# Decoder attention pass: both logits ahead of the guard's transform, a second key buffer, context energy on TensorE and variance on ScalarE

## The reference

```python
x = _layernorm(x + _L0_attn_ref(x), axis=-1)                     # autocorrelation, top 7 lags of 2048
x = _layernorm(x + _L0_xattn_ref(ctx_4096, ctx_4096, x), axis=-1)
x = _layernorm(x + _L0_ffn_ref(x, W_base, gate_W, A, B), axis=-1)

# _L0_xattn_ref(key, value, query)
sim = jnp.einsum('ncs,nds->ncd', key, query) * KC ** (-0.5)      # KC = 256
sim = jax.nn.softmax(sim, axis=1)
context = jnp.einsum('ncd,nds->ncs', sim, value)

# _L0_ffn_ref: a dense product and a mixture of low-rank experts
out = xf @ W_base.T + _moe_lora(xf, gate_W, A, B)                # 8 experts, rank 8, top 2
```

## Time and profile before

| | us |
|---|---|
| median of three runs | 2191.81 |
| the profiled execution | 2195.65 |
| its span, first to last instruction | 2193.8 |
| attention, up to the reading of the guard's flag | about 721 |

### The profile page before, as it was taken

One profiled execution on the slowest core, in us unless ns is written; L12 is line 12 of the kernel. 1 busy time (PEld: TensorE's weight loads), 2 busy tenths in 40 slices (PEclk: granted clock), 3 DMA queues, 4 the chain that ended last, 5 costly groups with the idle time before them and its releaser, 6 DMA issues.

```text
span 2193.8 us, 27988 instructions
## 1 busy us (share of the span) xinstructions
PE 1990.9 (91%) x11232; PEld 1056.9 (48%) x11232; DVE 988.7 (45%) x2182; ACT 511.9 (23%) x691; POOL 296.7 (14%) x418
## 2 busy tenths in 40 slices
PE   1878878878888699999999999999999999999998
PEld 1655645555555344444444444444444444444443
DVE  3788878888887652232223222232223222232222
ACT  4445444544442540010001000010001000110000
POOL 1242243243242320000000000000000000000000
PEclk9999999998999799999999999999999999999999
DMA  7588678778866752232223322232223322232220
GB/s 250 135 220 256 215 205 241 245 198 233 251 184 191 256 158 58 59 105 65 57 57 91 81 58 57 65 103 62 57 57 96 76 57 57 71 100 59 57 58 39
DMA packets 288907, 271.13 MB, mean 124 GB/s; under 512 B 261504, under 2 KB 261632, under 8 KB 265984
## 3 DMA queue, kind: packets, MB, share of 16 engines
q1 hardware_dynamic: 288832, 270.17, 42.4%
HBM read 138.02 MB, written 67.11 MB: 94 GB/s over the span
## 4 chain that ended last, share of the span: by engine, by line
PE 64%; ACT 1%; DMA 1%; POOL 1%; DVE 0%; issue 0%; ACTq 0%; SPq 0%; POOLq 0%
PE ps_y_f L1097 59%; PE ps_a_f L1116 1%; PE ps_y_f L1101 1%; PE ps_y_f L1102 1%; DMA chunk<-w_chunks 1%; PE ps_a_f L1117 1%; ACT w_hi_f L892 1%; POOL w_lo_f L875 0%; POOL chunk L874 0%; DVE w_lo_f L966 0%; PE ps_h_f L1124 0%; PE ps_t_f L1082 0%; DVE b_stack_f L1052 0%; ACT y_f L953 0%; ACT b_stack_f L950 0%
## 5 line engine op out<-in xcount | busy, mean ns | idle before, releaser
L1097 PE MATMUL ps_y_f<-w_hi_f,x_hi_f 128*128 128x512 f16 x2048 | 777.8, 380 | 9.9 <-POOL w_lo_f L875 7.4
L1097 PE MATMUL ps_y_f<-w_hi_f,x_lo_f 128*128 128x512 f16 x2048 | 778.0, 380 | 0.0
L1097 PE MATMUL ps_y_f<-w_lo_f,x_hi_f 128*128 128x512 f16 x2048 | 777.9, 380 | 0.0
L953 ACT ACTIVATE y_f<-y_f,nb_f,rs_f 128x2048 f32<-128x2048 f32 x32 | 67.0, 2093 | 1112.4 <-POOL nb_f L883 1112.4
L1097 PEld LDWEIGHTS ps_y_f<-w_hi_f,x_hi_f 128*128 128x128 f16 x2048 | 200.7, 98 | 246.8 <-POOL w_lo_f L875 9.6
L1097 PEld LDWEIGHTS ps_y_f<-w_hi_f,x_lo_f 128*128 128x128 f16 x2048 | 200.8, 98 | 242.6 <-issue 1.6
L1097 PEld LDWEIGHTS ps_y_f<-w_lo_f,x_hi_f 128*128 128x128 f16 x2048 | 200.7, 98 | 233.9 <-issue 1.4
L977 DVE SCALAR_TENSOR_TENSOR y_f<-ps_y_f,w_iscale,xn_f 128x512 f32<-128x512 f32 x64 | 46.6, 749 | 476.9 <-PE ps_y_f L1102 476.9
L977 DVE SCALAR_TENSOR_TENSOR y_f<-ps_y_f,w_iscale,xn 128x512 f32<-128x512 f32 x64 | 46.6, 748 | 447.9 <-PE ps_y_f L1102 447.9
L610 PE MATMUL ps_t_fast<-ident,xbuf_fast 128*128 128x128 f32 x512 | 95.5, 334 | 134.1 <-ACT xbuf_fast L413 116.3
L880 POOL TENSOR_TENSOR var_eps_f<-mv_f,columns 128x1 f32<-128x1 f32 x32 | 6.1, 191 | 1356.9 <-DVE mv_f L1065 1356.9
(11 more groups left out here) (146 smaller groups left out, 2055.2 us busy)
## 6 DMA issues: line engine op xcount, KB each, us to landing
cbuf_fast<-ctx_in SPq DMA_DIRECT2D x32, 1024.0 KB, 6.1
xbuf_fast<-x SPq DMA_DIRECT2D x32, 1024.0 KB, 8.8
x_scratch<-x2buf_fast SPq DMA_DIRECT2D x32, 1024.0 KB, 11.7
out<-y_f SPq DMA_DIRECT2D x32, 1024.0 KB, 4.1
xn<-w_chunks SPq DMA_DIRECT2D x16, 1024.0 KB, 8.4
xn<-x_scratch SPq DMA_DIRECT2D x16, 1024.0 KB, 4.8
xn_f<-x_scratch SPq DMA_DIRECT2D x16, 1024.0 KB, 4.8
chunk<-w_chunks SPq DMA_DIRECT2D x18, 512.0 KB, 5.6
```

The costliest lines, as they stand in the source:

```text
L953: nc.scalar.activation(y[parity][:], y[parity][:], ACT.Identity, bias=nb_[:, 0:1], scale=rs[:, 0:1]).then_inc(out_ready, 1)
L1097: nc.tensor.matmul(ps_y[j][:], xx[parity][:, k], ww[:, k, j * BANK:(j + 1) * BANK], start=(k == 0 and xx is x_hi and ww is w_hi), stop=False)
```

## The change

- The all-reduce of the context's squares (`reduce_context`, GpSimd) is replaced by one matmul with a matrix of ones (`context_energy`, TensorE, after the last bank of transposes). Its result of four columns lies in the PSUM bank of logits(1), so logits(1) waits for the scale.
- `k_both` has two buffers. The transposes of batch n + 2 stand at the end of slot n and wait for logits of batch n. In SP's queue the order of a slot is now store, weights, x, transposes with context n + 3.
- TensorE runs logits(0), logits(1), then the guard's transform and its way back.
- The statistics of x2 are no longer bn_stats. The context addition on VectorE also writes the sum of its output (`x2sum`), `x2_mean` makes the mean, ScalarE squares the centred rows with their sum (`spread2`), and GpSimd makes the normalisation from it, each row tile for itself (`norm2`, `normalise2`). For r = 1 this lies in the next slot.
- The first normalisation goes by row tile too: `norm_steps` twice, and `normalise1` for both tiles on ScalarE, the second one last in its slot.
- ScalarE's order after the banks: v_hi twice, normalise1(0), exponential(0), two squares of weights, exponential(1), four guard squares, normalise1(1).
- Some buffers share memory: `u_t` lies in `ag_raw`, one context buffer in two of the prefetched weight chunks. So the prefetches at the end of attention wait for the last transform and the last v_lo.

```diff
-                        transpose_keys(n + 1, 1 - parity, 0, 0)
-                        transpose_keys(n + 1, 1 - parity, 0, 1)
-                        for r in range(R):
-                            transpose_keys(n + 1, 1 - parity, 1, r)
-                            load_context(n + 2, r)
+                        store(n - 1, 1 - parity)
                         load_weights(n + 2)
-                        store(n - 1, 1 - parity)
                         load_x(n + 2, parity)
+                    for r in range(R):
+                        transpose_keys(n + 2, parity, 0, r)
+                    for r in range(R):
+                        transpose_keys(n + 2, parity, 1, r)
+                        load_context(n + 3, r)
...
                         if (part, r) == (0, 0):
-                            after(sp, sim_done, R * n)
+                            after(sp, sim_done, R * (n - 1))
...
+                def norm2(n, parity, r):
+                    at = slice(r, r + 1)
+                    pool.wait_ge(ssq2_ready, R * n + r + 1)
...
+                def normalise2(n, parity, r):
+                    pool.wait_ge(ln2_ready, R * n + r + 1)
...
+                    if is_batch(n - 1, nb):
+                        norm2(n - 1, 1 - parity, 1)
+                        normalise2(n - 1, 1 - parity, 1)
+                    if cur and n < nb - 1:
+                        norm2(n, parity, 0)
+                        normalise2(n, parity, 0)
+                    fold(0)
+                    norm1(0)
+                    fold(1)
+                    norm1(1)
...
+                    def spread2(n, parity, r):
+                        act.wait_ge(mean2_ready, R * n + r + 1)
+                        after(act, ssq2_ready, R * n + r)
+                        nc.scalar.activation(junk2[:], x2buf[parity][:, r], ACT.Square, bias=nmean2[parity][:, r:r + 1],
+                                             accum_out=ssq2[parity][:, r:r + 1]).then_inc(ssq2_ready, 1)
...
+                        if j == 1 and is_batch(n - 1, nb):
+                            spread2(n - 1, other, 1)
+                        if j == 5 and cur:
+                            spread2(n, parity, 0)
...
                                                    xbuf[parity][:, r, b * BANK:(b + 1) * BANK], ALU.mult,
-                                                   ALU.add).then_inc(ctx_added, 1)
-                            if j:
-                                x2_stats(j - 1)
+                                                   ALU.add, accum_out=x2sum[:, j:j + 1]).then_inc(ctx_added, 1)
+                            if j == NBANK:
+                                x2_mean(0)
...
                     softmax_max(0)
                     x_stats(1)
+                    guard_lags(0)
                     softmax_norm(0)
-                    guard_lags(0)
+                    softmax_max(1)
                     value_low(1)
-                    softmax_max(1)
                     softmax_norm(1)
...
+                    def context_energy():
...
+                            pe.wait_ge(sumsq_done, PIECES * (n + 3))
...
+                            nc.tensor.matmul(sumall, ones[:], sumsq[parity][:], start=True, stop=True).then_inc(sumall_done, 1)
...
                         pe.wait_ge(t_free, TQ * (n + 2))
+                        if n2:
+                            pe.wait_ge(scale_ready, n + 3)
+                        logits(1)
+
                         for evac in (evac_even, evac_odd):
...
                             ins.then_inc(fwd_done, 1)
-                        logits(1)
```

More of the change, by code:

```diff
@@ L46 @@
 AG = ER + EXPERTS
-EPS4_AT, EPS_AT, MINUS_ONE, MINUS_HALF = range(4)
+EPS4_AT, EPS_AT, MINUS_ONE, MINUS_HALF, ONE_LTH = range(5)
 GUARD_GAP = 110.0
@@ L140, in attention_pass @@
         q_hi, q_lo = sb("q_hi", [P, KT, C], F16), sb("q_lo", [P, KT, C], F16)
-        k_both = sb("k_both", [P, KT, 2, C], F16)
+        k_both = [sb(f"k_both{i}", [P, KT, 2, C], F16) for i in range(2)]
         p_hi, p_lo = sb("p_hi", [P, R, C], F16), sb("p_lo", [P, R, C], F16)
@@ L164, in attention_pass @@
         sumsq = [sb(f"sumsq{i}", [P, PIECES], F32) for i in range(2)]
-        sumall = [sb(f"sumall{i}", [P, PIECES], F32) for i in range(2)]
         scale = [sb(f"scale{i}", [P, 1], F32) for i in range(2)]
@@ L354, in slot @@
-                    if cur and not (isinstance(n, int) and n == nb - 1):
-                        pool.wait_ge(ln2_ready, n + 1)
-                        settle(1)
-                        for r in range(R):
-                            g.tensor_scalar(x2buf[parity][:, r], x2buf[parity][:, r], rs2[:, r:r + 1], nb2[:, r:r + 1], ALU.mult,
-                                            ALU.add).then_inc(x2_ready, 1)
-                    if isinstance(n, int) and n == nb - 1:
-                        pool.wait_ge(w_summed, 1)
+                            pool.wait_ge(mv1_ready, R * (n + 2) + r + 1)
@@ L435, in value_high @@
                             act.wait_ge(scale_ready, n + 3)
[L436 removed]
+                            nc.scalar.activation(v_hi[parity][:, r], cbuf[r][:], ACT.Copy, scale=scale[parity][:]).then_inc(vhi_done, 1)
                     def guard_squares(m):
@@ L444, in slot @@
                     value_high(0)
-                    guard_squares(0)
                     value_high(1)
-                    for m in range(1, 4):
-                        guard_squares(m)
-                    softmax_exp(0)
-                    if isinstance(n, int) and n == -2:
-                        square_weights(0)
-                        square_weights(1)
-                    normalise1()
-                    softmax_exp(1)
+                    normalise1(0)
+                    softmax_exp(0)
+                    square_weights(0)
+                    square_weights(1)
+                    softmax_exp(1)
+                    for m in range(4):
+                        guard_squares(m)
+                    normalise1(1)
                 batch_slots(act, None, nb, slot, 0)
@@ L523, in value_low @@
                             dve.wait_ge(vhi_done, R * (n + 2) + r + 1)
-                            v.scalar_tensor_tensor(v_lo[parity][:, r], cbuf[:, r], scale[parity][:], v_hi[parity][:, r], ALU.mult,
+                            v.scalar_tensor_tensor(v_lo[parity][:, r], cbuf[r][:], scale[parity][:], v_hi[parity][:, r], ALU.mult,
                                                    ALU.subtract).then_inc(vlo_done, 1)
@@ L638, in logits @@
                             k = i // 3
-                            ins = nc.tensor.matmul(ps_s[r][:, 0:C], qq[:, k, r * P:(r + 1) * P], k_both[:, k, part, :],
+                            ins = nc.tensor.matmul(ps_s[r][:, 0:C], qq[:, k, r * P:(r + 1) * P], k_both[other][:, k, part, :],
                                                    start=(i == 0), stop=(i == 3 * KT - 1))
```

158 lines of the change are left out of this document (77 added, 81 removed).

## The result

The changed kernel took **2077.1 us** (median of 4 runs, 2073.45 to 2080.91), the kernel before 2191.99 beside it: a ratio of 0.947, 95% interval 0.945 to 0.949. The profiled execution took 2076.6 us, 2074.7 of it span; that is what stands against the earlier trace rows.

What follows compares the result with a forecast made beforehand. No engine was full; TensorE waited for x's normalisation, held by GpSimd's all-reduce. Batches 63, start 16, last batches 3, less 4.4 at the end, made 78 us: 2118, less 3.8 to the median, 2114 us (range 2083 to 2162).

Steps and rivals of the forecast that it cites:

- The step that failed: TensorE's tail: a 3.0 us pause before the transform's fourth group, then 1.2 GHz, the batch ending at T+36.9.
- my table: Predicted times within one attention batch, T counting from TensorE's first transpose; with 0.6 us for hops, 37.5 us a batch.
- rival (a): TensorE's tail: ScalarE 1 us earlier, pause below 2.11 us, clock does not fall; 35.8 us a batch, 2090; chance 0.20.
- the start: Start of attention: first full batch begins at 58 instead of 74.4, 16 us won (bounds 9.5 and 18).
- The end: End of attention: weights' all-reduce, now first of its kind, 9.51 instead of 5.76, plus 0.6 for the square: 4.4 lost.
- worth 0 itself: Second key buffer: worth 0 itself as TensorE never waits for keys; it brings context rows some microseconds earlier.
- VectorE's relief: VectorE loses eight bn_stats of 0.6 us; slow clock and waits for VectorE made 3.5 us a batch.
- the context part: Contexts and transposes at the head of a batch: TensorE sets them, 15.5 us instead of 19.0.
- my last two terms: Last two batches without x work, 3 us won, and the end of attention, 4.4 us lost.
- Rival (c): GpSimd's long instructions lock VectorE out of copies and additions: at most 6.45 us a batch, 2204; chance 0.04.
- Rival (d): Loads of x land later, near 11.5 us, and the wait for the first rows stays: 2191.8 as before; chance 0.04.
- Rival (b): Context rows, weight squares and small GpSimd steps delay ScalarE by 2.5 us a batch: 40 us, 2149; chance 0.22.

Runs made afterwards that it cites:

- a_pause3: Kernel after with a ScalarE copy of 1344 columns (1.36 us) ahead of the first guard square: 2107.8 us, ratio 0.960.
- a_ctxfirst: Kernel after with the next context rows' load ahead of the v_lo transpose in SP's queue, key transposes waiting for the batch before: 2072.7 us, ratio 0.943.
- b_energy: Kernel before with one part alone: a TensorE matmul of ones replaces GpSimd's all-reduce in each batch: 2186.9 us, ratio 0.996.
- a_bnstats: Kernel after with x2's variance by VectorE's bn_stats again, no summing addition and no ScalarE squares for it: 2132.0 us, ratio 0.972.
- a_fwd_between: Kernel after with TensorE's transform back between logits(0) and logits(1), and ScalarE's guard squares back around the second v_hi: 2081.6 us, ratio 0.948.
- g1: Kernel after with ScalarE's two weight squares ahead of v_hi, and VectorE's maximum(1) ahead of guard lags and p(0): 2067.5 us, ratio 0.942.
- g4: Kernel after with transform between logits, weight squares ahead of v_hi, guard squares behind it, both x statistics ahead of v_lo, context loads ahead of key transposes: 2069.1 us.
- g2: As g1, with VectorE's v_lo(1) also moved ahead of maximum(1) and x's second statistics: 2097.0 us, ratio 0.955.
- a_late_square: Kernel after with one more ScalarE copy (1024 columns, about 1.05 us) ahead of the first guard square: 2100.1 us, ratio 0.956.
- a_onekey: Kernel after with one key buffer, so a batch's key transposes wait for logits(1) of the batch before: 2153.2 us, ratio 0.980.
- a_allreduce: Kernel after with GpSimd's all-reduce back at the head of its slot and no matmul of ones: 2365.7 us, ratio 1.078.

## Why the prediction was wrong

**The step that failed** is in the tail: "TensorE idles from 28.6 to about 31.6, 3.0 us, more than the 2.11 of the row, hence at 1.2 GHz". The pause was 1.64 us and the rate stayed. The groups before it ended 0.6 us later than in my table (T+29.2), and the first square let TensorE go on 0.8 us earlier (T+30.8). So 1.4 us of error in a chain of some thirty durations decided here between two outcomes 1.7 us a batch apart. I had read one row of a pause and its rate. The timeline of TensorE before held more, and they put 1.6 us on the side of full rate:

```profile
364.83 1.87 PE L679 MATMUL ps_g_fast<-inv_fast,power_fast 128*128 128x512 bf16 x4 [2.77 <-DVE g_lags L492]
...
529.50 1.02 PE L679 MATMUL ps_g_fast<-inv_fast,power_fast 128*128 128x512 bf16 x4 [1.65 <-DVE g_lags L492]
...
615.02 1.02 PE L679 MATMUL ps_g_fast<-inv_fast,power_fast 128*128 128x512 bf16 x4 [1.61 <-DVE g_lags L492]
```

The excess of 3.2 us a batch (37.5 against 34.3) lies almost wholly in this step. From TensorE's going on to the batch's end my table has 5.3 us and the trace 3.3: 2.0 for the rate. (The terms that I wrote there add up to 36.6, not to the 36.9 of the text, so 0.3 of the 2.0 is an error of addition.) The earlier square makes 0.8, and 0.6 are the hops that I added to the table and that it did not need; less 0.2, because the one batch that did fall lifts the mean from 34.1 to 34.3. a_pause3, whose pause was 2.85 us, shows what the step was worth: 36.4 us a batch, 36.8 where the rate fell. Even there the fourth group of the transform ran at full rate (1.05 to 1.10 us, where I had 1.7), and only the last eight matmuls were slow.

The outcome was that of rival (a), at 0.20, but not by its cause. GpSimd's small steps did not slip in ahead of v_lo(0); the square came early because a handful of durations were each a little shorter. The rival was priced too low as well: its 1.7 us are the clock alone, without the microsecond that it names itself. With both it would have been 2114 - 14 x 2.7 = 2076. That this is the measured time is luck, since the start and the end were off too.

14 times 3.2 is 45 us, more than the miss of 37. **What made up for part of it** is the start: 64.7 against a forecast of 58, so 9.7 us won instead of 16, close to the lower bound that I gave. I had named the second batch's context rows as what would hold it, and undersized them: they landed at 34.2 and 40.5 us (I had "near 35"), each behind a key transpose of 3.0 and 5.6 us in SP's queue. a_ctxfirst gave 3.4 of the 6.3 us back; the rest I can't place. The end was mis-sized the other way. The all-reduce of the weights is now the first of the kernel, and it was still a short one:

```profile
598.09 0.40 POOL L371 PARTITION_ALL_REDUCE w_total_all_fast<-w_total_fast  x1 [5.58 <-issue]
```

5.58 us of setting up, as in the second row, not the 9.51 of the first. So to be first in the program does not by itself cost 9.51 us; why the one at 23 us does stays open. From the last full batch's start to the last step of the weights' scale, which ends attention's work, went 53.8 us instead of 56.6: 2.8 won, where my last two terms made 1.4 lost. In sum: 9.7 + 14 x 7.7 + 2.8 = 120, less 1.3 us by which the part behind attention is longer, is the 119 between the spans. That is 41 us more than my 78. The other 4 lie in the step from the profiled run to the median: I took off 3.8 because the profiled run before lay above its median, and the one after lay 0.5 below its own.

**The cause of the gain** I had told too simply. I took GpSimd's all-reduce as the reason of the wait; b_energy removed it and a batch stayed at 41.9. I called the second key buffer "worth 0 itself"; taken away it costs 5.6 us a batch. That TensorE never waits for keys is true. I also wrote that the buffer brings the context rows earlier, but gave that no price, and the view of waits before has one, 300 to 620 us:

```profile
ACT junk_fast L391 <- DMA cbuf_fast<-ctx_in: 37.4, 14, 4.8
```

That is ScalarE waiting for context rows, some 5 us a batch. In the whole sum it did no harm, because the table for the changed kernel had the rows early. VectorE's relief was priced at 3.5 us a batch together with the clock, all of it in the context part. a_bnstats says 3.9, but 1.2 of it lie in the context part, 1.2 in the longer pause of the tail and some 1.5 in the rate behind it. So the gain is shown to need the second key buffer, VectorE's relief and the all-reduce's removal together. The swap in the order of SP's queue and the normalisation by row tile were not taken away by themselves, and the second key buffer was not tried on b_energy.

**What held.** The context part is TensorE's at 15.9 us (15.5). The summing addition costs VectorE 0.08 us for reading the accumulator beside an unchanged 0.75, where I had taken 0.1. Rival (c) fell: GpSimd's 2.05 us over x2 ran from 345.69 in the midst of copies and additions of 0.69 and 0.75 us, as the Trainium skill's rule has it (SBUF — State Buffer, Who interferes with whom); v_lo(0) with its two SBUF inputs did hold GpSimd, 2.17 us instead of 0.2. My p_hi row was no example of that side, since p_hi reads only one tensor in SBUF. The trace before has a true one: v_lo, begun at 445.33 beside a fold of GpSimd begun at 444.72, took 3.88 us instead of 2.35. In the timelines of GpSimd and VectorE after:

```profile
345.69 2.05 POOL L334 TENSOR_SCALAR x2buf_fast<-x2buf_fast,rs_fast,nb_fast 128x2048 f32<-128x2048 f32 x1
```

```profile
345.92 0.69 DVE L501 TENSOR_TENSOR q_lo_fast<-ps_t_fast,q_hi_fast 128x512 f16<-128x512 f32 x1
...
347.35 0.75 DVE L522 SCALAR_TENSOR_TENSOR x2buf_fast<-ps_c_fast,iscale_fast,xbuf_fast 128x512 f32<-128x512 f32 x1 [0.74 <-PE ps_c_fast L643]
348.02 0.08 DVE L522 DVE_READ_ACCUMULATOR x2buf_fast<-ps_c_fast,iscale_fast,xbuf_fast 128x1 f32 x1
```

and before:

```profile
444.72 2.35 POOL L323 TENSOR_TENSOR u_rows_fast<-xbuf_fast 128x1024 bf16<-128x1024 f32 x1
```

```profile
445.33 3.88 DVE L524 SCALAR_TENSOR_TENSOR v_lo_fast<-cbuf_fast,scale_fast,v_hi_fast 128x2048 f16<-128x2048 f32 x1
```

Rival (d) fell too: loads of x land after a median of 7.8 us, no later than before:

```profile
DMA to landing us min/median/max: 4.7/7.8/12.4
```

Rival (b) had the right suspects (context rows, weight squares), but here ScalarE waits for context rows 0.7 us a batch (4.9 in seven); they took over as soon as the tail was mended, in a_fwd_between, g1 and g4.

## What to carry to other kernels

When a wait is removed, follow every queue behind the engine that waits least visibly: here the same all-reduce was worth 0.4% in one order of the queues and 13 points in the other, and the trace of the second shows SP's queue carrying its delay to the loads of x. A long table of durations ends with an error of a microsecond or so; where an outcome jumps within that error, as the clock does, look up every row of the trace that bears on the jump, and give both sides near equal chances instead of one. Test the parts of a change by taking each away from the whole, not by adding it to the old kernel alone.

## What the hardware showed

- The rate after a pause is not told by that pause alone. Batches with half rate in the last matmuls, by the pause ahead of them: in the kernel after, none of 13 with 1.63 us and the one with 2.33; in a_ctxfirst one of 13 with 1.63, and not the one with 2.02; in g2 three of ten with 1.93 to 1.95 and all four with 2.10 to 2.70; in a_late_square 8 of 14 with 2.58 (one of them 2.80); in a_pause3 10 of 14 with 2.85; in a_bnstats all 14 with 2.81. In a_onekey the pause was again 1.63 us in all but one batch and the rate fell in 8 of 14, with other pauses of about 2.5 us in its context part. What decides it stays open.
- A fall costs 1.1 to 1.5 us a batch here (35.7 against 36.8 in a_pause3, 35.1 against 36.6 in a_late_square). The records of the last eight matmuls are longer by 1.6 us (1.89 + 1.75 against 1.04 + 1.03).
- GpSimd's all-reduce has a record of 0.44 us, but 5.8 to 9.5 us pass ahead of it and 6.8 to 9.4 behind it when other GpSimd instructions stand on both sides (the kernel before and a_allreduce). Between two all-reduces in a row there is no such pause: in the kernel after, the one at 599.98 begins 1.49 us after the one at 598.09 has ended.
